# Token halves for the last image's expert scatter, products laid out by group, and new engine orders

## The chip, the cores and the metric

One core of a Trainium2 chip runs the whole program in one launch. The metric is device time in microseconds (us), lower is better. TensorE does matrix products and transposes, VectorE, ScalarE and GpSimd (POOL in the rows) everything else, SyncE issues the DMAs.

## The reference

Four images x of 16 x 16 tokens and 128 channels go through two layers. The first is a deformable attention block. The second is an attention over the tokens with a choice of segments, and then the part that this change touches, a product-key expert layer. Cut to what matters:

```
# second layer, per image: t is 256 tokens x 128 channels, 8 heads
q  = layernorm_per_head(t_ln @ Wq.T + bq)                # 8 heads x 64
s0 = l2norm(q[..., :32]) @ l2norm(keys0).T               # 64 scores
s1 = l2norm(q[..., 32:]) @ l2norm(keys1).T               # 64 scores
sc0, ix0 = top_k(s0, 16);  sc1, ix1 = top_k(s1, 16)
fs, pos  = top_k(all sums sc0 + sc1, 16)                 # 16 chosen pairs
fi = (all sums ix0 + ix1)[pos]                           # expert number, 0 to 126
w  = softmax(fs)
act = gelu(t_ln . expert_down[fi])
t  = t + sum over heads and chosen of (act * w) * expert_up[fi]
```

Expert numbers are sums of two indices below 64, so only 128 experts occur.

## The kernel before

Each engine has its own in-order list of steps in `ORDERS`; a step has a name and an image, as N3a.2. A string `BANKS` gives each PSUM result its bank, in the order in which TensorE makes them. Engines meet through semaphores (a bank full, a bank free, a tile ready). The steps A and F of an image are the first layer and the attention of the second, the steps N its expert layer. The lists interleave the expert layer of image b with the front of image b+1 and b+2. An image has 256 tokens in two halves t = 0, 1 of 128.

The expert layer of an image, in the order of its data:

- N0a, N0h (halves 0, 1): queries, their squares (ScalarE), variances (VectorE), the power -0.5 (POOL, L1573). N0b, N0d: normalized queries, transposed. N0c, N0e: key scores (TensorE L775), copied to S (ScalarE L1045). N0f, N0g: norms.
- N1_0 to N1_3: VectorE finds the best 16 of 64 with MAX8, MATCH_REPLACE8 and FIND_INDEX8.
- N2p, N2q, N2a to N2f: sums, exponentials and the choice of 16 (halves 0, 0, 0, 1, 1, 1 on VectorE in N2a, N2b, N2c, N2d, N2e, N2f). `chosen` ends N2c and N2f with the sum, its reciprocal (L1388) and that times `W_SCALE` = 2^15 (L1389). POOL's `merge` puts weights and expert numbers into 27 slots per head and multiplies the weights by the scaled reciprocal (L1620), in N2c and N2f.
- N3a: TensorE transposes both halves' slots into banks wT and eT (8 transposes, 4 heads by 27 slots = 108 rows), once `slots_ready` counts both halves. ScalarE copies them to W2 (float16) and eT (uint16). VectorE takes the low 2 and the high 5 bits of the expert number (L1419, L1420), the float16 remainder of the weights (L1425), four masks for the low bits (L1428), and the products of weights and masks, R (L1432).
- N3b: the one-hots OH for the 32 values of the high bits, 28 on VectorE (L1437) and 4 on POOL (L1647), each over all 512 columns (2 chunks of heads, 2 halves, 4 x 32 tokens).
- N5a, N5b: the scatter, 128 small products each, OH by R (TensorE L839), into banks G0 and G1, one per token half. VectorE multiplies each with the activations of N4 into `prod` (L1442).
- N6a, N6b: 4 products with expert_up (TensorE L850), copy (ScalarE L1098), transpose, add and output (VectorE L1459), DMA.

So in the last image no other work is left after N2f.3 but this chain. The layout of `prod` decides how VectorE writes and how TensorE reads:

```
prod = masked[...].rearrange("p (l t q g) -> p l t q g", l=LO, t=NT, q=4)
# VectorE writes element (g, q, l) of half t; TensorE reads prod[:, lo], 256 elements
```

VectorE's, ScalarE's and POOL's operand tiles for the masks share SBUF: `lom` lies in `cands`, R in `weights`, `prod` in `masked`.

Of the kernel before, what the change touches and what calls it, by code (L numbers as in the profile page):

```python
# [31 lines left out]
NT = 2
# [87 lines left out]
    "scalar": """A0b.0 A1a.0 A2c.0 A2d.0 A3a.0 A1b.0 A3b.0 A3c.0 A4.0 A0b.1 F5b.0 A1a.1 F5c.0 F6b.0 F7a.0 F7b.0 A2c.1  # L120
        F8a.0 F8b.0 A1b.1 A2d.1 F9a.0 A3a.1 A3b.1 A3c.1 A4.1 A0b.2 F8c.0 F10a.0 F10b.0 F11t.0 A1a.2 F11b.0 F5b.1
        F12.0 F5c.1 N0a.0 F6b.1 N0h.0 N0b.0 N0c.0 F7a.1 F7b.1 N0d.0 F8a.1 F8b.1 A2c.2 F8c.1 N2p.0 A2d.2 F9a.1
        N0e.0 A3a.2 A3b.2 A3c.2 N2q.0 A1b.2 F10a.1 A4.2 F10b.1 F11t.1 F11b.1 N3a.0 F5b.2 F12.1 F5c.2 N0a.1 N0h.1
# [1598 lines left out]
```

## Time and profile before

| | us |
|---|---|
| median of 3 runs | 472.86 (471.47 to 474.82) |
| profiled execution, its own time | 472.43 |
| its span in the trace | 470.6 |
| mean granted TensorE clock, share of full | 0.675 |
| VectorE busy | 356.8 |
| TensorE busy | 296.5 |
| POOL busy | 220.8 |
| ScalarE busy | 137.3 |

The time of the profiled execution is 1.8 us more than its span. Busy times are sums over an engine's instructions; what an engine waits for is read from the chain and from the idle times.

### The profile page before, as it was taken

What the parts mean: (1) busy time and instruction counts of PE and PEld (TensorE: products, weight loads), DVE (VectorE), ACT (ScalarE), POOL (GpSimd) and SP (SyncE); (2) the same over time, 40 slices, a digit from 0 to 9 for tenths busy, and PEclk for the clock granted to TensorE, in tenths of its full rate; (3) what the DMA queues carried; (4) which work ended last, traced back from release to release, by engine and by line L of the source; (5) the groups of instructions that cost most, each with busy time, mean ns of one, the idle gap of its engine ahead of it and who ended that gap; (6) DMA issues with size and microseconds to landing.
All of it is one profiled execution on the core that took longest, in us unless ns stands there. A gap on an engine that the chain in (4) does not pass through costs nothing.

```text
span 470.6 us, 7700 instructions
## 1 busy us (share of the span) xinstructions
PE 296.5 (63%) x2233; PEld 219.8 (47%) x2233; DVE 356.8 (76%) x2124; ACT 137.3 (29%) x320; POOL 220.8 (47%) x407
## 2 busy tenths in 40 slices
PE   3074365886551485999957777998346579241196
PEld 1043144455340343699734445896122378231194
DVE  2858337227999989689999789999997896995811
ACT  3043232636320236261224544224043202031000
POOL 6229922395262187368455645031633920486300
PEclk9997577857685577575695975558758656575555
DMA  6000000000000000000000000000000000000000
GB/s 211 0 0 1 1 1 0 1 1 0 2 0 1 1 2 1 1 3 2 1 1 1 13 1 0 2 3 1 1 1 12 0 2 1 1 2 11 0 1 13
DMA packets 1633, 3.50 MB, mean 7 GB/s; under 512 B 180, under 2 KB 1205, under 8 KB 1592
## 3 DMA queue, kind: packets, MB, share of 16 engines
q1 hardware_dynamic: 1592, 3.01, 1.8%
q8 instruction: 18, 0.29, 0.3%
q14 instruction: 23, 0.19, 0.1%
HBM read 2.49 MB, written 0.52 MB: 6 GB/s over the span
## 4 chain that ended last, share of the span: by engine, by line
DVE 49%; PE 33%; ACT 7%; issue 5%; POOL 5%; DVEq 0%; ACTq 0%; POOLq 0%
PE bank L839 9%; DVE cands L1376 4%; DVE segmax L1201 4%; PE bank L520 4%; DVE onehot L1437 3%; DVE Sx L1320 3%; PE bank L755 3%; PE bank L775 3%; DVE i L1326 3%; DVE i L1327 3%; DVE c L1373 3%; DVE vraw L1323 2%; DVE rtm L1193 2%; DVE vraw L1317 2%; PE bank L608 2%
## 5 line engine op out<-in xcount | busy, mean ns | idle before, releaser
L839 PE MATMUL bank<-weights,onehot 108*128 108x16 f16 x1024 | 68.6, 216 | 18.5 <-DVE onehot L1437 13.0
L839 PEld LDWEIGHTS bank<-weights,onehot 108*128 108x128 f16 x1024 | 68.7, 175 | 19.4 <-DVE onehot L1437 13.5
L1584 POOL TENSOR_TENSOR inv<-nrm,mhalf 128x16 f32<-128x16 f32 x8 | 24.2, 3019 | 46.9 <-DVE nrm L1333 46.8
L454 POOL TENSOR_TENSOR taps<-qpad,wa 128x128 f32<-128x128 f32 x96 | 35.9, 425 | 17.4 <-ACT qpad L892 17.4
L1497 POOL TENSOR_TENSOR rstd<-veps,mhalf 128x2 f32<-128x2 f32 x16 | 11.7, 729 | 44.0 <-DVE veps L1123 43.7
L1647 POOL TENSOR_SCALAR onehot<-eT 108x512 f16<-108x512 uint16 x16 | 30.2, 1888 | 4.2 <-DVE eT L1420 3.5
L1437 DVE TENSOR_SCALAR onehot<-eT 108x512 f16<-108x512 uint16 x112 | 28.1, 327 | 0.0
L1326 DVE FIND_INDEX8 i<-vraw,S 128x8 uint16<-128x64 f32 x128 | 28.0, 219 | 0.0
L1327 DVE FIND_INDEX8 i<-vraw,Sx 128x8 uint16<-128x64 f32 x128 | 28.0, 219 | 0.0
L708 PE MATMUL bank<-qB,kE 32*128 32x256 f32 x128 | 16.3, 663 | 18.0 <-ACT PT L1003 10.1
L775 PE MATMUL bank<-KB,qsT 128*128 128x256 f32 x64 | 24.4, 548 | 3.5 <-ACT qsT L1035 3.5
L1320 DVE MATCH_REPLACE8 Sx<-vraw,S 128x64 f32<-128x64 f32 x128 | 25.1, 209 | 0.0
L1573 POOL TENSOR_TENSOR qrstd<-ssq,mhalf 128x8 f32<-128x8 f32 x8 | 17.7, 2212 | 14.7 <-DVE ssq L1285 14.7
L1376 DVE MATCH_REPLACE8 cands<-c,cands 128x54 f32<-128x54 f32 x128 | 23.7, 199 | 0.0
L520 PE MATMUL bank<-wa,hat 128*128 128x128 f32 x24 | 7.4, 406 | 24.8 <-ACT hat L877 24.6
L1317 DVE MAX8 vraw<-S 128x8 f32<-128x64 f32 x128 | 17.7, 213 | 6.3 <-ACT S L1045 6.3
L1201 DVE TENSOR_REDUCE segmax<-bank 128x32 f32<-128x512 f32 x32 | 19.8, 681 | 2.5 <-PE bank L678 2.4
L775 PEld LDWEIGHTS bank<-KB,qsT 128*128 128x128 f32 x64 | 17.2, 283 | 8.1 <-ACT qsT L1035 4.9
L1602 POOL TENSOR_TENSOR weights<-ab 128x64 f32<-128x64 f32 (+3 forms) x40 | 12.6, 348 | 17.9 <-ACT ab L1065 17.9
L1529 POOL TENSOR_TENSOR taps<-taps 128x1536 f32<-128x1536 f32 (+3 forms) x12 | 20.6, 1714 | 0.6
L1442 DVE TENSOR_TENSOR masked<-bank,act 128x512 f32<-128x512 f32 x8 | 8.4, 1072 | 16.0 <-PE bank L839 15.9
L708 PEld LDWEIGHTS bank<-qB,kE 32*128 32x128 f32 x128 | 10.0, 319 | 22.1 <-issue 12.0
(224 smaller groups left out, 775.9 us busy)
## 6 DMA issues: line engine op xcount, KB each, us to landing
wa<-wa_dram SPq DMA_DIRECT2D x1, 747.5 KB, 4.6
wb<-wb_dram SPq DMA_DIRECT2D x1, 707.0 KB, 5.7
x_sb<-x_dram SPq DMA_DIRECT2D x4, 128.0 KB, 4.0
out_dram<-eT SPq DMA_DIRECT2D x4, 128.0 KB, 1.7
onehot<-ws_dram SPq DMA_DIRECT2D x1, 448.0 KB, 6.3
bq_row<-rows_dram SPq DMA_DIRECT2D x1, 0.5 KB
onehot<-rows_dram SPq DMA_DIRECT2D x1, 13.5 KB
```

The lines of the kernel that those rows point to most:

```text
L454: ins = eng.tensor_tensor(tv[:, :, :, ky, kx:kx + n], q, dw[:, ky, kx:kx + n].unsqueeze(1).unsqueeze(1).broadcast_to([P, G8, G8, n]), ALU. ...
L708: last = mm(banks[i][:, kc * N:kc * N + N], kE[r, j, kc * P:kc * P + P], qB[r, j, :], start=True, stop=True)
L775: last = mm(o[:, i * 256:i * 256 + 256], qsT[:, t, 2 * j + i, :], KB[:, :], start=True, stop=True)
L839: last = mm(o[:, g * 16:g * 16 + 16], OHv[:, c * NT + t, g], Rv[:, c, t, g, s], start=(c == 0 and s == 0), stop=(c == NCH - 1 and s == 1))
L1201: freed(v.tensor_reduce(segmax[:, t * H + i:t * H + H:4, :], o[:, :].rearrange("p (g n) -> p g n", n=SEG), X, ALU.max), job, b)
L1317: last = v.max(vt[:, g, 0:8], sv[:, g, :])
L1320: last = v.match_replace(sx[:, g, :], vt[:, g, 0:8], sv[:, g, :], MARK)
L1326: v.max_index(it[:, g, 0:8], vt[:, g, 0:8], sv[:, g, :])
L1327: last = v.max_index(it[:, g, 8:16], vt[:, g, 8:16], sx[:, g, :])
L1376: last = v.match_replace(dst[:, g, :], c8[:, g, i, :], src[:, g, :], MARK)
L1437: last = v.tensor_scalar(OH[0:KC, :, :, hi, :], hi_view(eT), float(LO * hi), None, ALU.is_equal)
L1647: last = g_.tensor_scalar(OH[0:KC, :, :, hi, :], hi_view(eT), float(LO * hi), None, ALU.is_equal)
```

## The change

1. In the last image N3a and N3b work on token half 0 alone, and new steps N3h (transposes, copies, bits, masks, R) and N3i (one-hots) on half 1. N3a.3 waits for one half's slots, N5a.3 for half 0's one-hots, N5b.3 for half 1's. R is then made with 8 instructions a half (each of the two float16 parts alone) instead of 4 in all. The other images keep whole steps.
2. The scale 2^15 moves from its own VectorE instruction into ScalarE's copy (the function Identity with a scale for Copy) and into the subtraction, which becomes one scalar_tensor_tensor.
3. `prod` is laid out by half, group and (q, l): VectorE writes 512 elements in a row, TensorE reads with a step of 16 elements.
4. All four orders and the banks are new.

```diff
+    "N3a": ["wT", "eT"], "N3h": ["wT1", "eT1"],
     "N4": ["I"],
     "N5a": ["G0"], "N5b": ["G1"],
...
-        F12.2 N0a.2 N0h.2 F6a.3 F6b.3 N0b.2 F6c.3 N0f.2 N0c.2 N0d.2 N0e.2 N5a.1 F7a.3 F7b.3 N5b.1 F8a.3 N4.2
...
-        F12.3 N0a.3 N0h.3 N0b.3 N0c.3 N0f.3 N5a.2 N0d.3 N0e.3 N0g.3 N5b.2 N6a.2 N4.3 N6b.2 N3a.3 N5a.3 N5b.3
-        N6a.3 N6b.3""".split(),
...
-        N6a.1 F11t.3 F11b.3 N3a.2 F12.3 N0a.3 N0h.3 N0b.3 N0c.3 N0d.3 N0e.3 N2p.3 N2q.3 N6a.2 N4.3 N3a.3 N6a.3""".split(),
...
-        N3a.2 N0a.3 N0h.3 N0b.3 N3b.2 N1_0.3 N0d.3 N1_1.3 N1_2.3 N0f.3 N5a.2 N1_3.3 N0g.3 N2a.3 N5b.2 N2d.3
-        N2b.3 N2c.3 N2e.3 N2f.3 N6b.2 N3a.3 N3b.3 N5a.3 N5b.3 N6b.3""".split(),
...
-        N0f.2 N2a.2 N0g.2 N2c.2 N2d.2 N2f.2 F11c.3 N0a.3 N0h.3 N3b.2 N0f.3 N0g.3 N2a.3 N2d.3 N2c.3 N2f.3 N3b.3""".split(),
...
+        F12.2 N0a.2 F6a.3 N0h.2 F6b.3 N0b.2 F6c.3 N0c.2 N0f.2 N5a.1 F7a.3 N0d.2 F7b.3 N0e.2 N5b.1 F8a.3 F8b.3
...
+        F12.3 N0a.3 N0h.3 N0b.3 N0c.3 N5a.2 N0d.3 N0f.3 N0e.3 N5b.2 N0g.3 N4.3 N6a.2 N6b.2 N3a.3 N3h.3 N5a.3
+        N5b.3 N6a.3 N6b.3""".split(),
...
+        F10b.3 F11t.3 F11b.3 N3a.2 F12.3 N0a.3 N0h.3 N0b.3 N0c.3 N0d.3 N0e.3 N2p.3 N2q.3 N4.3 N6a.2 N3a.3 N3h.3
+        N6a.3""".split(),
...
+        N0a.3 N0h.3 N0b.3 N3b.2 N1_0.3 N0d.3 N1_1.3 N1_2.3 N0f.3 N1_3.3 N0g.3 N5a.2 N5b.2 N2a.3 N2b.3 N2d.3
+        N2c.3 N6b.2 N2e.3 N2f.3 N3a.3 N3b.3 N3h.3 N3i.3 N5a.3 N5b.3 N6b.3""".split(),
...
+        F7b.3 N2a.2 N2c.2 N0g.2 N2d.2 N2f.2 F11c.3 N0a.3 N3b.2 N0h.3 N0f.3 N0g.3 N2a.3 N2d.3 N2c.3 N2f.3 N3b.3
+        N3i.3""".split(),
...
-        prod = masked[:, 0:NT * 32 * 4 * LO].rearrange("p (l t q g) -> p l t q g", l=LO, t=NT, q=4)
+        prod = masked[:, 0:NT * 32 * 4 * LO].rearrange("p (t g e) -> p t g e", t=NT, g=32)
...
+        def first_halves(b):
+
+            return list(range(NT)) if b < B - 1 else [0]
+
+        def part(ap, halves):
+
+            return ap if len(halves) == NT else ap.rearrange("p (c t n) -> p c t n", c=NCH, t=NT)[:, :, halves[0], :]
+
+        def masks(unit, hi, halves):
+
+            e = eT[0:KC, 2, :]
+            if len(halves) == NT:
+                return unit.tensor_scalar(OH[0:KC, :, :, hi, :], e.rearrange("p (n q g) -> p n q g", n=NCH * NT, q=4),
+                                          float(LO * hi), None, ALU.is_equal)
+            t = halves[0]
+            return unit.tensor_scalar(OH[0:KC, t:NCH * NT:NT, :, hi, :],
+                                      e.rearrange("p (n q g) -> p n q g", n=NCH * NT, q=4)[:, t:NCH * NT:NT],
+                                      float(LO * hi), None, ALU.is_equal)
...
+                read_out(pe, "tT", b)
...
+            def slot_transposes(b, halves, job):
+                pe.wait_ge(slots_ready, NT * b + halves[-1] + 1)
+                for kind, src in (("w", wn[:, :, :]), ("e", slots[:, 1, :, :])):
+                    transposes(kind + job, b, [
+                        ((c * NT + t) * P, src[:, t * H + c * HC:t * H + (c + 1) * HC, :].rearrange("p h s -> p (h s)"))
+                        for c in range(NCH) for t in halves])
+
             def N3a(b):
-                pe.wait_ge(slots_ready, NT * (b + 1))
-                for job, src in (("wT", wn[:, :, :]), ("eT", slots[:, 1, :, :])):
-                    transposes(job, b, [((c * NT + t) * P,
-                                         src[:, t * H + c * HC:t * H + (c + 1) * HC, :].rearrange("p h s -> p (h s)"))
-                                        for c in range(NCH) for t in range(NT)])
+                slot_transposes(b, first_halves(b), "T")
+
+            def N3h(b):
+                slot_transposes(b, [1], "T1")
...
             def N5b(b):
+                if b == B - 1:
+                    pe.wait_ge(onehot_dve_ready, b + 2)
+                    pe.wait_ge(onehot_pool_ready, b + 2)
                 scatter(b, 1)
...
+                pv = prod[:, :, :, :].rearrange("p t g (q l) -> p l t q g", q=4)
                 for lo in range(LO):
-                    last = mm(o[:, 0:N], up[:, lo, :], prod[:, lo], start=(lo == 0), stop=(lo == LO - 1))
+                    last = mm(o[:, 0:N], up[:, lo, :], pv[:, lo], start=(lo == 0), stop=(lo == LO - 1))
...
+            def slot_copies(b, halves, job):
+                o = full(ac, "w" + job, b)
+                link(fn(part(W2[0:KC, 0, :], halves), part(o[0:KC, :], halves), ACT.Identity, scale=W_SCALE))
+                o = full(ac, "e" + job, b)
+                freed(fn(part(eT[0:KC, 0, :], halves), part(o[0:KC, :], halves), ACT.Copy), "e" + job, b)
...
-                o = full(ac, "wT", b)
-                link(fn(W2[0:KC, 0, :], o[0:KC, :], ACT.Copy))
-                o = full(ac, "eT", b)
-                freed(fn(eT[0:KC, 0, :], o[0:KC, :], ACT.Copy), "eT", b)
+                slot_copies(b, first_halves(b), "T")
+
+            def N3h(b):
+                slot_copies(b, [1], "T1")
...
-                link(v.reciprocal(zs[:, 1, h], zs[:, 0, h]))
-                v.tensor_scalar(zs[:, 2, h], zs[:, 1, h], W_SCALE, None, ALU.mult).then_inc(wem_ready, 1)
+                v.reciprocal(zs[:, 1, h], zs[:, 0, h]).then_inc(wem_ready, 1)
...
+            def slot_rows(b, halves, job):
+                n = b + halves[-1] if b == B - 1 else b
+                read_out(dve, "e" + job, b)
+                v.tensor_scalar(part(eT[0:KC, 1, :], halves), part(eT[0:KC, 0, :], halves), LO - 1, None, ALU.bitwise_and)
+                v.tensor_scalar(part(eT[0:KC, 2, :], halves), part(eT[0:KC, 0, :], halves), E - LO, None,
+                                ALU.bitwise_and).then_inc(eT_ready, 1)
+
+                o = full(dve, "w" + job, b)
+                dve.wait_ge(act_chain, n + 1)
+                freed(v.scalar_tensor_tensor(part(W2[0:KC, 1, :], halves), part(o[0:KC, :], halves), W_SCALE,
+                                             part(W2[0:KC, 0, :], halves), ALU.mult, ALU.subtract), "w" + job, b)
+                dve.wait_ge(eT_ready, n + 1)
+                for lo in range(LO):
+                    last = v.tensor_scalar(part(lom[0:KC, lo, :], halves), part(eT[0:KC, 1, :], halves), float(lo), None,
+                                           ALU.is_equal)
+                link(last)
+                read_out(dve, "w" + job, b)
+                for lo in range(LO):
+                    if len(halves) == NT:
+                        v.tensor_tensor(R[0:KC, :, lo, :], W2[0:KC, :, :],
+                                        lom[0:KC, lo, :].unsqueeze(1).broadcast_to([KC, 2, NCH * N]), ALU.mult)
+                    else:
+                        for s in range(2):
+                            v.tensor_tensor(part(R[0:KC, s, lo, :], halves), part(W2[0:KC, s, :], halves),
+                                            part(lom[0:KC, lo, :], halves), ALU.mult)
...
+                slot_rows(b, first_halves(b), "T")
+
+            def N3h(b):
+                slot_rows(b, [1], "T1")
...
+                    last = masks(v, hi, first_halves(b))
+                last.then_inc(onehot_dve_ready, 1)
+
+            def N3i(b):
+                for hi in range(POOL_HI, HI):
+                    last = masks(v, hi, [1])
                 last.then_inc(onehot_dve_ready, 1)
...
                 freed(v.tensor_tensor(
-                    prod[:, :, t, :, :].rearrange("p l q g -> p g q l"),
-                    o[:, :].rearrange("p (g q l) -> p g q l", g=32, q=4), act[:, t, :, :, :], ALU.mult), f"G{t}", b)
+                    prod[:, t, :, :], o[:, :].rearrange("p (g e) -> p g e", g=32),
+                    act[:, t, :, :, :].rearrange("p g q l -> p g (q l)"), ALU.mult), f"G{t}", b)
...
-                                 zs[:, 2, h].unsqueeze(2).broadcast_to([P, H, SLOTS]), ALU.mult)\
+                                 zs[:, 1, h].unsqueeze(2).broadcast_to([P, H, SLOTS]), ALU.mult)\
...
+                    last = masks(g_, hi, first_halves(b))
+                last.then_inc(onehot_pool_ready, 1)
+
+            def N3i(b):
+                pool.wait_ge(eT_ready, b + 2)
+                for hi in range(0, POOL_HI):
+                    last = masks(g_, hi, [1])
                 last.then_inc(onehot_pool_ready, 1)
```

Entries of a list that an engine has no code for (as A2b.0 on POOL) do nothing. The other differences of the lists are exchanges of near neighbours: POOL takes N0a.0 and N0h.0 before the taps of image 2, ScalarE does A1a.2 after F12.0, and TensorE does N0d.2 and N0e.2 behind N5a.1, where both stood before it.

## Rows read from the trace of the kernel before

**Rows 1.** The page of the whole span: slices and chain by engine

```profile
DVE  2858337227999989689999789999997896995811
PEclk9997577857685577575695975558758656575555
...
DVE 49%; PE 33%; ACT 7%; issue 5%; POOL 5%; DVEq 0%; ACTq 0%; POOLq 0%
```

**Rows 2.** The timeline, all engines, end of the last image's choice (start, us, what)

```profile
424.63 1.32 POOL L1620 TENSOR_TENSOR wn<-slots,zs 128x216 f32<-128x216 f32 x1
...
426.45 0.17 DVE L1389 TENSOR_SCALAR zs<-zs 128x8 f32<-128x8 f32 x1
426.53 0.42 DVE L1459 TENSOR_TENSOR eT<-bank,t 128x256 f32<-128x256 f32 x1
```

**Rows 3.** The timeline, all engines, from the last slots to the end

```profile
429.21 0.55 POOL L1620 TENSOR_TENSOR wn<-slots,zs 128x216 f32<-128x216 f32 x1
...
431.03 0.60 ACT L1082 ACTIVATE W<-bank 108x512 f16<-108x512 f32 x1 [9.70 <-PE bank L520]
...
432.56 0.29 DVE L1419 TENSOR_SCALAR eT<-eT 108x512 uint16<-108x512 uint16 x1 [5.60 <-ACT eT L1084]
...
433.21 6.54 POOL L1647 TENSOR_SCALAR onehot<-eT 108x512 f16<-108x512 uint16 x4 [3.46 <-DVE eT L1420]
...
438.20 6.55 DVE L1437 TENSOR_SCALAR onehot<-eT 108x512 f16<-108x512 uint16 x28
...
444.80 16.98 PE L839 MATMUL bank<-weights,onehot 108*128 108x16 f16 x256 [13.04 <-DVE onehot L1437]
...
461.82 1.02 DVE L1442 TENSOR_TENSOR masked<-bank,act 128x512 f32<-128x512 f32 x1 [7.07 <-PE bank L839]
...
462.95 3.75 PE L850 MATMUL bank<-masked,up 128*128 128x256 f32 x8 [1.16 <-issue]
466.74 0.38 ACT L1098 ACTIVATE W<-bank 128x256 f32<-128x256 f32 x1 [34.28 <-PE bank L850]
...
467.97 0.42 DVE L1459 TENSOR_TENSOR eT<-bank,t 128x256 f32<-128x256 f32 x1 [5.12 <-PE bank L520]
```

**Rows 4.** Windows of N3a.1, N3b.2, N3b.1: busy us (x count) of PE, PEld, DVE, ACT, POOL

```profile
271.30:275.80 4.50, 3.56 (x7) 1.19 (x8) 4.45 (x12) 2.63 (x6) 0.00 (x0) 0.75 0.00 2
...
367.40:373.20 5.80, 4.76 (x17) 3.77 (x17) 5.80 (x30) 2.18 (x4) 5.80 (x2) 0.56 0.00 0
...
280.00:289.10 9.10, 8.04 (x26) 5.88 (x25) 9.10 (x30) 2.99 (x5) 7.33 (x5) 0.52 0.00 0
```

**Rows 5.** The timeline of VectorE in N3a.1 and just before N3a.2

```profile
272.33 0.89 DVE L1428 TENSOR_SCALAR cands<-eT 108x512 f16<-108x512 uint16 x4
273.25 2.50 DVE L1432 TENSOR_TENSOR weights<-W,cands 108x1024 f16<-108x1024 f16 x4
...
358.22 0.17 DVE L1122 TENSOR_SCALAR negmean<-mv 128x2 f32<-128x2 f32 x1
358.30 0.16 DVE L1123 TENSOR_SCALAR veps<-mv 128x2 f32<-128x2 f32 x1
```

**Rows 6.** Groups by line and shape, VectorE: count, then busy us, mean ns

```profile
L1442 DVE TENSOR_TENSOR masked<-bank,act 128x512 f32<-128x512 f32 x8 | 8.4, 1072 | 16.0 <-PE bank L839 15.9
L1291 DVE TENSOR_TENSOR queries<-bank,qrstd 128x512 f32<-128x512 f32 x8 | 5.5, 683 | 1.1 <-POOL qrstd L1573 1.1
...
L1389 DVE TENSOR_SCALAR zs<-zs 128x8 f32<-128x8 f32 x8 | 1.5, 182 | 0.3
```

**Rows 7.** The timelines of POOL, TensorE and VectorE around the scatter of image 2

```profile
368.61 10.58 POOL L1647 TENSOR_SCALAR onehot<-eT 108x512 f16<-108x512 uint16 x4
...
379.29 8.56 PE L839 MATMUL bank<-weights,onehot 108*128 108x16 f16 x128 [5.51 <-issue]
...
392.46 1.11 DVE L1317 MAX8 vraw<-S 128x8 f32<-128x64 f32 x8 [4.50 <-ACT S L1045]
```

**Rows 8.** Groups by line and shape, TensorE's weight loads

```profile
L839 PEld LDWEIGHTS bank<-weights,onehot 108*128 108x128 f16 x1024 | 68.7, 175 | 19.4 <-DVE onehot L1437 13.5 <-issue 5.8
```

More of the change, by code:

```diff
@@ L120 @@
[L120 to L123, printed above, removed]
-        A0b.3 F6b.2 N0b.1 N0c.1 N0d.1 A1a.3 N4.0 F7a.2 N0e.1 F7b.2 F8a.2 F8b.2 F8c.2 F9a.2 A2c.3 A2d.3 N2p.1
-        A3a.3 A3b.3 A3c.3 F10a.2 F10b.2 N2q.1 A1b.3 F11t.2 N6a.0 A4.3 F11b.2 F5b.3 N3a.1 F12.2 F5c.3 N0a.2 N0h.2
-        F6b.3 N0b.2 N0c.2 N0d.2 N4.1 F7a.3 F7b.3 N0e.2 F8a.3 N4.2 F8b.3 F9a.3 N2p.2 N2q.2 F10a.3 F8c.3 F10b.3
-        N6a.1 F11t.3 F11b.3 N3a.2 F12.3 N0a.3 N0h.3 N0b.3 N0c.3 N0d.3 N0e.3 N2p.3 N2q.3 N6a.2 N4.3 N3a.3 N6a.3""".split(),
@@ new lines @@
+    "vector": """A0a.0 NB.0 A2c.0 A3a.0 A0a.1 F5a.0 NS.0 F6a.0 F6c.0 F7b.0 A2c.1 F8b.0 F9b.0 F9a.0 F9c.0 A0a.2 F9d.0
+        F5a.1 F11a.0 F11c.0 N0a.0 F6a.1 N0b.0 N0h.0 F6c.1 N0d.0 N1_0.0 N1_1.0 F7b.1 N0f.0 N0g.0 N1_2.0 A2c.2
+        N2a.0 F8b.1 N1_3.0 F9b.1 A3a.1 F9a.1 F9c.1 N2b.0 F9d.1 N2d.0 N2c.0 N2e.0 N2f.0 F11a.1 A0a.3 F11c.1 F5a.2
+        N3a.0 N3b.0 N0a.1 A3a.2 F6a.2 N0h.1 N0b.1 N0d.1 F6c.2 N1_0.1 N1_1.1 N0f.1 N1_2.1 F7b.2 N2a.1 A2c.3 N2b.1
+        N5a.0 N5b.0 F8b.2 F9b.2 F9a.2 F9c.2 N2c.1 F9d.2 N0g.1 N1_3.1 N2d.1 N2e.1 A3a.3 N2f.1 F11a.2 N6b.0 F5a.3
+        F11c.2 N3a.1 N0a.2 F6a.3 N0b.2 N3b.1 N0h.2 N1_0.2 F6c.3 N0d.2 N1_1.2 N5a.1 F7b.3 N0f.2 N1_2.2 N2a.2
+        N2b.2 F8b.3 N5b.1 F9b.3 F9a.3 F9c.3 N2c.2 N0g.2 F9d.3 N1_3.2 N2d.2 N2e.2 N2f.2 F11a.3 N6b.1 F11c.3 N3a.2
+        N0a.3 N0h.3 N0b.3 N3b.2 N1_0.3 N0d.3 N1_1.3 N1_2.3 N0f.3 N1_3.3 N0g.3 N5a.2 N5b.2 N2a.3 N2b.3 N2d.3
+        N2c.3 N6b.2 N2e.3 N2f.3 N3a.3 N3b.3 N3h.3 N3i.3 N5a.3 N5b.3 N6b.3""".split(),
@@ L860, in _ @@
                   "F10b": F10b, "F11a": F11a, "F11t": F11t, "F11b": F11b, "F11c": F11c, "F12": F12, "NS": NS,
-                  "N0a": N0a, "N0h": N0h, "N0b": N0b, "N0c": N0c, "N0d": N0d, "N0e": N0e, "N0f": N0f, "N0g": N0g, "N3a":
-                  N3a, "N4": N4, "N5a": N5a, "N5b": N5b, "N6a": N6a, "N6b": N6b}
+                  "N0a": N0a, "N0h": N0h, "N0b": N0b, "N0c": N0c, "N0d": N0d, "N0e": N0e, "N0f": N0f, "N0g": N0g, "N3a": N3a, "N3h": N3h, "N4": N4, "N5a": N5a, "N5b": N5b, "N6a": N6a, "N6b": N6b}
             for s, b in schedule("tensor"):
@@ L1468, in _ @@
                   N1_1, "N1_2": N1_2, "N1_3": N1_3, "N2a": N2a, "N2b": N2b, "N2c": N2c, "N2d": N2d, "N2e": N2e,
-                  "N2f": N2f, "N3a": N3a, "N3b": N3b, "N5a": N5a, "N5b": N5b, "N6b": N6b, "NB": setup_rows}
+                  "N2f": N2f, "N3a": N3a, "N3b": N3b, "N3h": N3h, "N3i": N3i, "N5a": N5a, "N5b": N5b, "N6b": N6b, "NB": setup_rows}
             for s, b in schedule("vector"):
```

72 lines of the change are left out of this document (26 added, 46 removed).

## The prediction

> **What bounds the kernel now.** I read the chain of waits first, then the timeline of the last 50 us, then windows and groups for prices. The chain gives VectorE 49% of the span and TensorE 33%; VectorE's slices are nearly full from the tenth on and empty again in the last four [rows 1]. So there are three regimes. Up to about 100 us a latency chain through image 0's front, then some 320 us in which VectorE is almost always at work, then the tail, where only the last image is left.
>
> The tail is a queue of steps of which each waits for the whole of the one before. VectorE ends N2f.3 at 426.62 (426.45 + 0.17) [rows 2]. POOL's last weights are there at 429.76, VectorE starts N3a.3 at 432.56, ends the one-hots at 444.75, TensorE scatters for 16.98 us alone, from 444.80 to 461.78, and product, up-projection and output end at 468.39 [rows 3]. From N2f.3's end to the scatter's end it is 461.78 - 426.62 = 35.16 us. During VectorE's 12.2 us TensorE is idle, during the scatter VectorE is, and the first half's weights lay ready from 425.95 (424.63 + 1.32) [rows 2]. TensorE's granted clock is about half in these slices [rows 1], the lower of its levels; nothing in the change raises it, so I keep the scatter's price.
>
> **The change, part by part.** T is the end of N2f.3 on VectorE, 426.62 before.
>
> *Start of half 0.* Between the last weights and N3a.3 lay 432.56 - 429.76 = 2.80 us for 8 transposes and two ScalarE copies of 512 [rows 3]. With 4 transposes and copies of 256 (0.38 as L1098 instead of 0.60 as L1082 [rows 3], so 0.44 less for two) and about 0.6 less transposing (half of the 1.27 us from 429.76 until the first copy starts at 431.03) it is 1.8. Half 0's weights come 0.67 before T, and N6b.2, 0.42 long [rows 2], now stands between N2c.3 and N2e.3, so 1.1 before T. VectorE starts half 0 at T + 0.7 and waits that long for it. The bounds are 0.1 (transposes all hidden) and 2.1 (nothing gets shorter and N6b.2 adds no lead).
>
> *VectorE's work for one half.* Undisturbed, the whole N3a takes 4.45 us [rows 4], of it 0.92 for the four low masks (272.33 to 273.25) and 2.42 for the four R [rows 5]; the 28 one-hots take 5.8 us at most, 0.205 each (the window of N3b.2, of which 0.06 are neighbours) [rows 4]. What an instruction costs without elements is near 0.08, the distance of two two-element ones [rows 5]. Then a one-hot of 256 columns is 0.08 + 0.0625 = 0.142, 28 of them 4.0; a low mask 0.155, four 0.6; an R of 256 instead of 1,024 elements 0.08 + 0.13 = 0.21, eight 1.7; the bits and the remainder, 1.03 whole (271.30 [rows 4] to 272.33 [rows 5]), about 0.65. That is 7.0 us, against half of 10.2 = 5.1 if there were no fixed cost, and 10.2 if nothing shrank. I take 7.0, because the two-element rows show the fixed cost.
>
> *POOL beside it.* N3b.1's window is 9.1 us with POOL's four masks in it, N3b.2's, 5.8, has the same 28 one-hots on VectorE and little of POOL's finished [rows 4]; before, N3a.3 and N3b.3 together took 12.2 with 6.54 us of POOL masks beside them [rows 3], 2.0 more than 10.2. So POOL's masks cost VectorE 2 to 3.3 us whole. For half 0 POOL now has its merge of half 1 (3.1 us, from T to 429.76) and half masks beside VectorE. I add 1.5, between 0.5 and 4.2. N5a.3 starts at T + 0.7 + 7.0 + 1.5 = T + 9.2.
>
> *The scatter.* 16.98 / 2 = 8.5 for half 0 [rows 3]. Half 1's work on VectorE, 7.0 + 1.0 beside POOL's second masks, begins at T + 9.2 and ends at T + 17.2, half 0's scatter at T + 17.7. So half 1 is hidden with only 0.5 us to spare, and N5b.3 ends at T + 26.2. Before it was T + 35.2. The split gives 9.0; with POOL's and the start's bounds 5 to 11.
>
> *Products.* L1442 takes 1.07 us; L1291, also one PSUM input, one SBUF input, 512 float32 and a result in a row, takes 0.683 [rows 6]. The difference, 0.39, is what the result's step costs, if it is the step. The last product is on the end of the path: 0.4. TensorE then reads `prod` with 64-byte steps, in L850's 3.75 us. OH (float16) is loaded with a step of 64 bytes too, 128 columns in 175 ns on average, most of it beside other work [rows 8]: such a load and its product together take 16.98 / 256 = 0.066 us [rows 3], far less than the 0.47 us of one L850 instruction (3.75 / 8) for 256 columns. I take zero, up to 3.75 if reads took twice as long.
>
> The Trainium skill (SBUF — State Buffer, Specifications) says that each access to a new 16-byte line pays a penalty and that two hits on a line are wanted. By it the write of the product becomes cheaper, which agrees with 1,072 against 683 ns, but all of TensorE's reads for N6a pay; no row here shows by how much for float32.
>
> *Scale.* L1389, 0.182 mean [rows 6], goes 8 times, 7 of them ahead of T; the eighth releases POOL. Identity for Copy and scalar_tensor_tensor for tensor_tensor process the same elements from the same places: nothing, up to 0.1 each.
>
> *Before T.* VectorE sheds 8 x 0.18 = 1.4 and the six products of images 0 to 2, 6 x 0.39 = 2.3, together 3.7. It is not always the limit (VectorE waits 4.5 us before N1_2.3 [rows 7], and waits elsewhere end with an engine that hasn't become faster), so I count half, 1.9, between 0 and 3.7.
>
> *Orders.* One exchange has a row. TensorE was idle 5.51 us before N5a.2 until POOL's last mask at 379.19, which stood behind N0h.3, and N0d.3 and N0e.3 queued behind that scatter; VectorE waited 4.50 us for their scores [rows 7]. Now POOL does N3b.2 before N0h.3. It can gain up to 4.5, or nothing where VectorE's own masks hold POOL up as they did (10.58 us for four [rows 7], against 7.33 of POOL in all in image 1's window [rows 4]); I take 1.0. N6b.2 ahead of T costs 0.4. For all other exchanges and banks I take 0, with -6 to +4: they move steps by a few places, and the removed waits in a full VectorE are only worth what VectorE idles.
>
> T moves from 426.6 by -1.9 - 1.0 + 0.4 = -2.5.
>
> **Sum.** 2.5 + 9.0 + 0.4 = 11.9 us. The profiled execution, 472.43, would become 460.5; it lies 0.4 below the median 472.86, so on the median it is 461.0.
>
> **The rivals.**
>
> *A. The lock.* POOL and VectorE don't slow each other but take turns. For it speaks that image 2's POOL masks took 10.58 us while VectorE made its own [rows 7]; against it, that in N3b.1 one-hots worth 5.7 us and 7.33 of POOL fitted into 9.1 [rows 4], where turns would need nearly 13. In turns half 0 needs 7.0 plus 3.3 of masks (half of 6.54) plus about 2.4 of merge, 4.2 more than I counted, and half 1 needs 10.3 against a scatter of 8.5, 1.8 more. Then 461.0 + 6.0 = 467.0. The Trainium skill (SBUF — State Buffer, Who interferes with whom) states this as a rule: an exclusive lock for a whole instruction, taken by tensor_scalar in its fast modes or by two SBUF inputs. The trace agrees that there is a price, not that all is serial.
>
> *B. Better orders.* VectorE's idle in the first 110 us and the 4.5 us go down by 4 more: 457.0. For it, every removed idle there counts; against, that stretch is a chain through all engines.
>
> *C. A shared wait.* N5a.3 or VectorE's half 0 waits for something of half 1, so the split gives nothing and the doubled fixed costs (2 x 7.0 - 10.2 = 3.8) fall due: 461.0 + 9.0 = 470.0 to 473.8. In the code N5a.3 waits for counts b+1 and N3a.3 for the first half, so this is unlikely; I put it at 471.
>
> *D. Strided reads.* N6a.3 doubles: 461.0 + 3.75 = 464.8.
>
> *E. Slower: scatters in VectorE's way.* In the new TensorE list N0d.2 and N0e.2 stand behind N5a.1 and F7a.3. A scatter is 8.5 us in which key scores queue, and the trace shows one such case, at 4.5 us of VectorE idle [rows 7]. If two scatters fall wholly into VectorE's way it is 461.0 + 17.0 = 478.0. It decides once N0e's scores are later than N1_1's end by more than 12 us in sum, 473. Against it, VectorE has N1_0.2 and N1_1.2, 128 searches and more, queued to cover one scatter.
>
> **How the numbers follow.** Forecast 0.62 (457.5 to 464.5), A 0.13, B 0.10, D 0.05, C 0.05, E 0.05. A tenth of the chance lies below about 457 and a tenth above 468, so the range is 455.5 to 468. A change of under 1% (4.7 us) can't be told from none here. Faster by over 1% means under 468.1: forecast, B, D and nearly all of A, 0.89. Within 1% are C and A's upper end, 0.07; slower by over 1% is E's larger part, 0.04.
>
> **What would show it.** Right: the scatter's first product within 8 to 10.5 us of N2f.3's end, 256 products without a gap over 0.5 us, POOL's masks of half 1 beside the first 128, L1442 near 0.68 us, no L1389, N6a.3 at 3.7 us, VectorE's wait before N1_2.3 shorter. Wrong: one-hots of 256 columns at over 0.2 us, a gap between the halves of the scatter, or a VectorE idle of several us at a place that had none in images 1 and 2.

## Result and the profile after

| | before | after |
|---|---|---|
| median of 4 runs, us | 473.58 (471.47 to 474.82) | 457.69 (457.07 to 460.12) |
| profiled execution, its own time | 472.43 | 460.12 |
| its span | 470.6 | 458.0 |

The ratio is 0.9679, with a 95% interval of 0.9626 to 0.9731: 15.2 us less than before (12.7 to 17.7). The profiled execution after is the longest of its four. In all comparisons the medians take every execution, and the ratios leave out one of e9's six, a slow one of 457.0 us at a lower granted clock; e8 has three slow ones of six, and its ratio fits all six.

The page after answers to [rows 1]. The first two lines are the span and VectorE's busy tenths, then the granted clock in tenths, then the chain by engine.

```profile
span 458.0 us, 7753 instructions
...
DVE  4828328225999998849999978999998699999950
...
PEclk9997556787567577555678589555785665665556
...
DVE 57%; PE 22%; POOL 7%; issue 7%; ACT 5%; DMA 0%; DVEq 0%; POOLq 0%; ACTq 0%
```

VectorE now has 57% of the chain and TensorE 22%, where it was 49% and 33%, so more of the chain that ended last runs over VectorE. VectorE's digits are near full up to the third slice from the end, and the last but one holds a 5, its work on half 1 beside the scatter. The granted clock of the last slices is 0.5 to 0.6, as before.

The timeline of the tail answers to [rows 2] and [rows 3]. T, the end of N2f.3 on VectorE, is 423.40 + 0.20 = 423.60.

```profile
421.27 0.55 POOL L1671 TENSOR_TENSOR wn<-slots,zs 128x216 f32<-128x216 f32 x1
...
421.58 1.15 DVE L1417 SCALAR_TENSOR_TENSOR masked<-cands,weights 128x864 f32<-128x864 f32 x1
...
423.08 0.38 ACT L1107 ACTIVATE eT<-bank 108x256 uint16<-108x256 f32 x1
423.40 0.20 DVE L1422 RECIPROCAL zs<-zs 128x8 f32<-128x8 f32 x1
423.56 0.23 DVE L1450 TENSOR_SCALAR eT<-eT 108x256 uint16<-108x256 uint16 x1
...
424.22 1.23 DVE L1460 TENSOR_SCALAR cands<-eT 108x256 f16<-108x256 uint16 x4
425.48 2.46 DVE L1470 TENSOR_TENSOR weights<-W,cands 108x256 f16<-108x256 f16 x8
...
426.95 3.83 POOL L495 TENSOR_SCALAR onehot<-eT 108x256 f16<-108x256 uint16 x4
...
427.86 4.82 DVE L495 TENSOR_SCALAR onehot<-eT 108x256 f16<-108x256 uint16 x28
...
432.60 0.22 DVE L1450 TENSOR_SCALAR eT<-eT 108x256 uint16<-108x256 uint16 x1
...
432.74 17.05 PE L867 MATMUL bank<-weights,onehot 108*128 108x16 f16 x256 [4.60 <-DVE onehot L495]
...
433.04 3.85 POOL L495 TENSOR_SCALAR onehot<-eT 108x256 f16<-108x256 uint16 x4 [2.26 <-DVE eT L1451]
433.20 0.85 DVE L1460 TENSOR_SCALAR cands<-eT 108x256 f16<-108x256 uint16 x4
434.09 2.06 DVE L1470 TENSOR_TENSOR weights<-W,cands 108x256 f16<-108x256 f16 x8
436.07 4.22 DVE L495 TENSOR_SCALAR onehot<-eT 108x256 f16<-108x256 uint16 x28
441.45 0.69 DVE L1493 TENSOR_TENSOR masked<-bank,act 128x512 f32<-128x512 f32 x1 [1.17 <-PE bank L867]
449.82 0.69 DVE L1493 TENSOR_TENSOR masked<-bank,act 128x512 f32<-128x512 f32 x1 [7.67 <-PE bank L867]
...
450.61 3.76 PE L879 MATMUL bank<-masked,up 128*128 128x256 f32 x8 [0.83 <-issue]
...
455.39 0.42 DVE L1510 TENSOR_TENSOR eT<-bank,t 128x256 f32<-128x256 f32 x1 [4.88 <-PE bank L538]
```

Read it as two interleaved queues. Half 0's expert numbers arrive in SBUF at 423.08 + 0.38 = 423.46, before T, so VectorE goes from the reciprocal straight into half 0 (423.56). Its one-hots end at 432.68, and TensorE begins its 256 products at 432.74. VectorE turns to half 1 at 432.60 and is done at 440.29. The 256 products then stand in one group without a gap to 449.79. L1493 for half 0 (it was L1442) waits 1.17 us for TensorE, so half 1 was hidden with about that to spare. From T the first product is at +9.1 (before +18.2), the end of the scatter at +26.2 (before +35.2). TensorE's products with `prod` at 64-byte steps (L879, it was L850) take 3.76 us in this tail, against 3.75 [rows 3]; in image 0 they take longer than before (last section).

The 9.0 us that left the tail up to the scatter's end are so made: 5.9 in which VectorE had waited from T until half 1's slots were merged, transposed and copied (432.56 - 426.62), and 3.1 of the 12.2 us of masks [rows 3].

The group of the product with the activations, which answers to the first of [rows 6]:

```profile
L1493 DVE TENSOR_TENSOR masked<-bank,act 128x512 f32<-128x512 f32 x8 | 5.3, 684 | 8.9 <-PE bank L867 8.8
```

1,072 ns has become 684, the price of L1291 beside it in [rows 6].

Image 2's one-hots, N3b.2, in the timeline of POOL and VectorE, which answer to [rows 7]:

```profile
365.78 7.08 POOL L492 TENSOR_SCALAR onehot<-eT 108x512 f16<-108x512 uint16 x4
...
366.45 8.58 DVE L492 TENSOR_SCALAR onehot<-eT 108x512 f16<-108x512 uint16 x28
```

POOL's masks now come first, and VectorE's wait of 4.50 us before N1_2.3 is gone. But VectorE's own 28 masks take 8.58 us. In the kernel before they took 5.74, and there it was POOL that stood, as its timeline and VectorE's show:

```profile
367.00 6.22 POOL L1573 TENSOR_TENSOR qrstd<-ssq,mhalf 128x8 f32<-128x8 f32 x1 [0.49 <-DVE ssq L1285]
...
367.44 5.74 DVE L1437 TENSOR_SCALAR onehot<-eT 108x512 f16<-108x512 uint16 x28
```

POOL's power, 1.64 us elsewhere, took 6.22 and ended at 373.22, with the last of VectorE's masks at 373.18, and POOL's four masks behind it took 10.58 [rows 7] instead of 6.54.

### The profile page after: what moved, and what is told of

Read it like the earlier page. It is cut to its first block, busy times and chain, and to the rows that moved or that the text cites. A ratio compares the mean times of both kernels' runs of the same rounds, so it can differ in the third digit from the quotient of the medians.

```text
span 458.0 us, 7753 instructions
## 1 busy us (share of the span) xinstructions
PE 310.4 (68%) x2233; PEld 230.4 (50%) x2233; DVE 360.6 (79%) x2163; ACT 141.3 (31%) x324; POOL 216.7 (47%) x411
## 4 chain that ended last, share of the span: by engine, by line
DVE 57%; PE 22%; POOL 7%; issue 7%; ACT 5%; DMA 0%; DVEq 0%; POOLq 0%; ACTq 0%
PE bank L867 7%; DVE Sx L1354 5%; DVE cands L1410 5%; DVE i L1360 5%; DVE i L1361 4%; DVE segmax L1235 4%; DVE onehot L492 4%; DVE vraw L1357 3%; DVE c L1407 3%; DVE vraw L1351 3%; PE bank L538 2%; DVE masked L1417 2%; DVE cands L1399 2%; DVE rtm L1227 2%; PE bank L794 2%
## 5 line engine op out<-in xcount | busy, mean ns | idle before, releaser
L794 PE MATMUL bank<-KB,qsT 128*128 128x256 f32 x64 | 25.7, 573 | 1.8 <-ACT qsT L1063 1.7
L1624 POOL TENSOR_TENSOR qrstd<-ssq,mhalf 128x8 f32<-128x8 f32 x8 | 13.6, 1704 | 27.3 <-DVE ssq L1319 27.2
L492 DVE TENSOR_SCALAR onehot<-eT 108x512 f16<-108x512 uint16 x84 | 23.7, 357 | 0.0
L492 POOL TENSOR_SCALAR onehot<-eT 108x512 f16<-108x512 uint16 x12 | 20.2, 1680 | 2.2 <-DVE eT L1451 1.6
L1648 POOL TENSOR_TENSOR ab<-v 128x256 f32<-128x256 f32 x8 | 5.4, 676 | 32.9 <-DVE v L1393 14.1
L1351 DVE MAX8 vraw<-S 128x8 f32<-128x64 f32 x128 | 17.7, 210 | 3.4 <-ACT S L1073 3.4
L1031 ACT ACTIVATE PT<-bank 128x512 f32<-128x512 f32 x32 | 16.3, 613 | 10.4 <-PE bank L727 10.4
L538 PEld LDWEIGHTS bank<-wa,hat 128*128 128x128 f32 x24 | 3.4, 196 | 30.7 <-ACT hat L905 30.7
L1357 DVE MAX8 vraw<-Sx 128x8 f32<-128x64 f32 x128 | 17.8, 211 | 0.6
```

The source lines that it names most:

```text
L492: return unit.tensor_scalar(OH[0:KC, :, :, hi, :], e.rearrange("p (n q g) -> p n q g", n=NCH * NT, q=4), float(LO * hi), None, ALU.is_equal)
L794: last = mm(o[:, i * 256:i * 256 + 256], qsT[:, t, 2 * j + i, :], KB[:, :], start=True, stop=True)
L1351: last = v.max(vt[:, g, 0:8], sv[:, g, :])
L1357: last = v.max(vt[:, g, 8:16], sx[:, g, :])
```

## Experiments

All were timed in rounds with the kernel before on the same chip, one chip for e1 to e4, one for e5 to e8 and one for e9 to e12, with the medians of before in that order. The ratio is to that kernel; 0.01 is 4.7 us. T and "from T" are read from the timeline of the profiled execution, T in us from the span's start: the distances are those of the first product of the scatter, its end, and the end of VectorE's last add.

| kernel | median, us | ratio (95%) | T | from T |
|---|---|---|---|---|
| before | 473.0, 474.2, 475.1 | 1 | 426.6 | 18.2, 35.2, 41.8 |
| after | 457.69 | 0.9679 (0.9626 to 0.9731) | 423.6 | 9.1, 26.2, 32.2 |
| e1 | 468.65 | 0.9865 (0.9818 to 0.9913) | 431.2 | 11.0, 28.0, 34.3 |
| e2 | 465.5 | 0.9832 (0.9774 to 0.9889) | 427.0 | 9.1, 26.2, 32.6 |
| e3 | 467.03 | 0.9828 (0.978 to 0.9876) | 422.2 | 18.2, 35.2, 41.3 |
| e4 | 469.51 | 0.9906 (0.9873 to 0.9939) | 427.3 | 18.2, 35.4, 41.7 |
| e5 | 462.07 | 0.9751 (0.971 to 0.9792) | 425.2 | 9.8, 26.8, 32.9 |
| e6 | 473.38 | 0.9978 (0.9945 to 1.0011) | 428.2 | 18.2, 35.3, 41.9 |
| e7 | 460.43 | 0.9694 (0.9649 to 0.9739) | 424.4 | 9.1, 26.1, 32.5 |
| e8 | 454.38 | 0.9574 (0.9522 to 0.9627) | 412.2 | 8.5, 25.6, 31.6 |
| e9 | 449.1 | 0.9456 (0.9422 to 0.9489) | 412.8 | 9.1, 26.2, 32.2 |
| e10 | 458.35 | 0.9644 (0.9606 to 0.9682) | 421.5 | 9.1, 26.2, 32.3 |
| e11 | 467.36 | 0.9849 (0.9811 to 0.9887) | 425.1 | 16.9, 34.0, 40.4 |
| e12, after again | 457.61 | 0.9634 (0.9599 to 0.9668) | 419.3 | 9.1, 26.2, 32.2 |

Two kinds of number stand in this table. The distances from T repeat within 0.2 us in kernels with the same tail. T itself doesn't: after, e12 and e3 are the same program up to T and have it at 423.6, 419.3 and 422.2, and before and e1 at 426.6 and 431.2. So the tail is read from the profile, and what lies ahead of T from the ratios of whole times.

**e1, the split alone**, with the orders, scale and products of before:

```diff
-  "vector": ... N2b.3 N2c.3 N2e.3 N2f.3 N6b.2 N3a.3 N3b.3 N5a.3 N5b.3 N6b.3
+  "vector": ... N2b.3 N2c.3 N2e.3 N2f.3 N6b.2 N3a.3 N3b.3 N3h.3 N3i.3 N5a.3 N5b.3 N6b.3
```

> The kernel before with the split of the last image alone: N3h and N3i added, all else (scale, product layout, orders, banks) as before, N6b.2 still behind N2f.3. Theory of the split: ScalarE's N3a.3 now has to wait until image 2's output is stored, which VectorE releases 0.3 us after T, so half 0 starts some 3 us later than in the changed kernel: 28.5 to 30 us from the end of N2f.3 (T) to the end of the scatter, where it was 35.2, a span of 464 to 466 us. Rival, the split alone is worth all of its 9 us: 461.6. Rival, the new orders carry the gain: the span stays within 2 us of 470.6.

It gained 6.4 us (4.1 to 8.6) and its scatter ends at T + 28.0, 7.1 earlier than before. VectorE enters N3a.3 only at T + 3.2. Its timeline says why:

```profile
431.57 0.33 SPq L509 DMA_DIRECT2D out_dram<-eT  x1
...
433.44 0.38 ACT L1100 ACTIVATE W<-bank 108x256 f16<-108x256 f32 x1 [7.34 <-DMA out_dram<-eT]
...
434.35 0.23 DVE L1446 TENSOR_SCALAR eT<-eT 108x256 uint16<-108x256 uint16 x1 [2.86 <-ACT eT L1102]
```

ScalarE's copy of half 0 (433.44) had waited 7.34 us, and what ended the wait is image 2's output going out (`out_dram<-eT`): the step's copies fill `eT` again, from which that output is read. With N6b.2 behind N2f.3, the output is late.

**e2, the split and N6b.2 moved** ahead of N2e.3:

```diff
-  "vector": ... N2c.3 N2e.3 N2f.3 N6b.2 N3a.3 N3b.3 N3h.3 ...
+  "vector": ... N2c.3 N6b.2 N2e.3 N2f.3 N3a.3 N3b.3 N3h.3 ...
```

> As the kernel with the split alone, but VectorE does N6b.2 right behind N2c.3. Theory of the split: T + 26.2 at the end of the scatter, less 0.4 for N6b.2 in front of T, a span of 462.0 (461 to 463). Rival, N6b.2's place doesn't matter: the same as the kernel with the split alone. Rival, the new orders carry the gain: above 467.

N3a.3 starts at T and the scatter ends at T + 26.2, as in the kernel after. So the moved step is a condition of the split: it is worth 1.8 us of the 9.0 behind T, less the 0.4 that it now takes ahead of T.

**e3, the kernel after without the split:**

```diff
-            return list(range(NT)) if b < B - 1 else [0]
+            return list(range(NT))
```

> The changed kernel without the split (N3a.3 and N3b.3 whole, N3h and N3i gone); scale, products, orders and banks are the new ones. Theory of the split: T as in the changed kernel, 423.7, the end of the scatter 34 to 35 us later, a span of 466 to 467.5. Rival, the orders carry the gain: 458 to 461.

```profile
428.81 6.54 POOL L488 TENSOR_SCALAR onehot<-eT 108x512 f16<-108x512 uint16 x4 [3.46 <-DVE eT L1444]
...
433.79 6.55 DVE L488 TENSOR_SCALAR onehot<-eT 108x512 f16<-108x512 uint16 x28
...
440.39 17.04 PE L860 MATMUL bank<-weights,onehot 108*128 108x16 f16 x256 [13.04 <-DVE onehot L488]
...
457.48 0.69 DVE L1486 TENSOR_TENSOR masked<-bank,act 128x512 f32<-128x512 f32 x1 [7.63 <-PE bank L860]
```

The queue of before is back: masks, then 256 products after all of them. The scatter ends at T + 35.2, 9.0 later than in the kernel after. By the ratios the split is worth 0.9828 - 0.9679, 7.0 us (3.6 to 10.4), here and 7.9 us (5.3 to 10.7) in e2. Both intervals hold 9.0; the 9.0 itself rests on the distances from T.

**e4, only the scale and the products** on top of before:

> The kernel before with the scale in ScalarE's copy and the products laid out by group, nothing else. By the prediction's terms: 0.4 from the last product and half of 3.7 us ahead of T, a span of 468.3 (466.5 to 470.2). Rival, all of the VectorE time that is saved counts: 466.5. Rival, the waits take it all: 470.2. TensorE's N6a.3 stays at 3.7 us; if reads with a step of 64 bytes were slow it would be 5 to 7.5.

4.4 us faster (2.9 to 6.0), nearly all of it ahead of T, since the tail is that of before but for 0.3 us from the scatter's end to the output's (6.3 for 6.6). N6a.3's reads at the new step take the same time, 3.78 us for 3.75, at a granted clock of 0.50 in both; N6a.0's, at 1.00, take 3.70 where they took 1.99.

**e5, all of the change but the new orders and banks** (N6b.2 still moved):

> The changed kernel with the orders and banks of the kernel before (N3h and N3i added at their places, N6b.2 behind N2c.3). Theory that the orders are worth little: split 8.6, scale and products 2.3, a span of 459.5 to 460.5, 1.5 to 2.5 above the changed kernel, most of it the 4.5 us wait of VectorE before N1_2.3 less what POOL's masks cost VectorE in N3b.2. Rival, the new orders lose time (VectorE is 3 us later until about 265 us in the changed kernel): 455 to 457. Rival, they carry much: above 463.

It lies 0.0072, 3.4 us, above the kernel after, with an uncertainty of 3.2 (the half-widths 0.0041 and 0.0053 added in squares); the intervals overlap a little. Its tail is 0.6 longer, and its timeline says why:

```profile
423.31 1.06 DVE L1413 SCALAR_TENSOR_TENSOR masked<-cands,weights 128x864 f32<-128x864 f32 x1
423.32 1.45 POOL L1667 TENSOR_TENSOR wn<-slots,zs 128x216 f32<-128x216 f32 x1
...
426.53 0.35 DVE L1446 TENSOR_SCALAR eT<-eT 108x256 uint16<-108x256 uint16 x1 [1.28 <-ACT eT L1103]
```

POOL's multiplication of half 0's weights begins in the same moment as VectorE's scalar_tensor_tensor with two SBUF inputs, and takes 1.45 us instead of the 0.55 that it takes in the kernel after (421.27), where it got ahead. The slots of half 0 come that much later, and N3a.3 waits 1.28 us.

**e6, POOL's masks ahead of N0h.3** in before and nothing else:

```diff
-  "gpsimd": ... F11c.3 N0a.3 N0h.3 N3b.2 N0f.3 ...
+  "gpsimd": ... F11c.3 N0a.3 N3b.2 N0h.3 N0f.3 ...
```

> The kernel before with one exchange in POOL's list: N3b.2 ahead of N0h.3. Theory: POOL's masks then run beside VectorE's, which take 8.6 instead of 5.7 us (+2.8), and the wait of 4.5 us before N1_2.3 goes: a span of 469.0 (468.5 to 469.5), 1.6 less. Rival, POOL stays locked out until VectorE is done: 470.6. Rival, all of the 4.5 us is won: 466.

0.9978 with 1 inside the interval: the 1.6 us that were expected can't be told from none, but the rival that all of the 4.5 is won is out. The wait before N1_2.3 is gone, 4.5 us, but N3b.2 costs 2.4 more:

```profile
369.78 6.98 POOL L1647 TENSOR_SCALAR onehot<-eT 108x512 f16<-108x512 uint16 x4
...
371.14 8.18 DVE L1437 TENSOR_SCALAR onehot<-eT 108x512 f16<-108x512 uint16 x28
```

**e7, the kernel after with the old layout of `prod`:**

> The changed kernel with the old layout of the products (VectorE writes with large steps, TensorE reads in a row). Theory: the write's step costs 0.37 us for each of 8 products, one of them in the tail, the others ahead of T where VectorE is nearly always the limit: +1.6 to +2.7 on 458.0. Rival, waits absorb all but the last: +0.4. N6a.3 stays at 3.76 us.

0.7 us above the kernel after, with an uncertainty of 3.3: it can't tell nothing from the whole 2.7 (0.4 in the tail and 2.3 ahead of it). TensorE's N6a.0 takes 2.22 us here, at a granted clock of 0.89.

**e8, no masks on POOL**, VectorE makes all 32 of each image (`POOL_HI = 0`, and POOL's waits and those on POOL go):

> The changed kernel without POOL's four one-hot masks: VectorE makes all 32. Theory of the contention: N3b.1 and N3b.2 on VectorE go from 8.6 us (28 beside POOL) to 32 x 0.205 = 6.6, N3b.0 from 6.5 to 6.6 but N3a.0 from 5.65 to 4.45, the halves of the last image from 4.8 and 4.2 to 4.5 each: about 5 us less work on VectorE ahead of T, a span of 453 to 456. Rival, POOL's masks are a help: 0.8 us more VectorE work per image, a span of 460 to 461.

```profile
416.27 4.42 DVE L495 TENSOR_SCALAR onehot<-eT 108x256 f16<-108x256 uint16 x32
...
423.51 4.44 DVE L495 TENSOR_SCALAR onehot<-eT 108x256 f16<-108x256 uint16 x32
```

All 32 one-hots of a half take VectorE 4.42 us alone; in the kernel after, 28 of them took 4.82 with POOL's four beside them. The ratio is 0.9574, 5.0 us (1.5 to 8.5) below the kernel after. Its six times fall into two groups, 447.8 to 453.2 and 455.6 to 456.1.

**e9, masks on POOL in the last image alone** (and the waits for them to match):

```diff
...
-                for hi in range(POOL_HI, HI):
+                for hi in range(POOL_HI if b == B - 1 else 0, HI):
...
             def N3b(b):
-                if b >= 1:
-                    full(pool, "G1", b - 1)
+                if b < B - 1:
+                    return
```

> The changed kernel with VectorE making all 32 one-hot masks in images 0 to 2, POOL its four only in the halves of the last image. Theory that the gain of dropping POOL's masks lies ahead of the tail: the end of N2f.3 as without any POOL masks, the tail 0.6 us longer (T + 26.1 at the end of the scatter), a time within 1 us of the kernel without POOL masks, some 454 to 455. Rival, the tail gives most of it: near the changed kernel, 457.5.

0.9456 (0.9422 to 0.9489): the fastest, 8.5 us (6.2 to 10.8) below the kernel after on the same chip (e12, 0.9634), and faster than both kernels. Five of its six times lie between 448.4 and 449.9, and the ratio is theirs; the sixth is 457.0. Against e8 the difference is unclear: e8's three shortest times, 447.8, 449.6 and 453.2, lie around e9's, its three others make its ratio larger, and by the tail e9 should be 0.6 us longer.

**e10, image 0's POOL masks later** in POOL's list, behind N0h.1:

```diff
-  "gpsimd": ... F11c.1 N3b.0 A0a.3 A0b.3 N0a.1 N0h.1 A2a.3 ...
+  "gpsimd": ... F11c.1 A0a.3 A0b.3 N0a.1 N0h.1 N3b.0 A2a.3 ...
```

> The changed kernel with N3b.0 later in POOL's list, behind N0h.1 instead of ahead of A0a.3; the masks stay. Theory of the queue: what dropping POOL's masks gives in image 0 is that image 3's layernorm (A0a.3, A0b.3) no longer waits behind 6.5 us of masks, so A1a.3 doesn't hold up TensorE's list; then 2 to 4 us less than the changed kernel, 454 to 456. Theory of the contention alone: VectorE's N3a.0 and N3b.0 go from 5.65 + 6.55 to 4.45 + 5.75, 2.0 us less, and N5a.0 has to wait for POOL until about 202 us, behind the 204 where it starts now: 455.7. Rival, the later masks hold up N5a.0 and the key scores behind it: 458 or more.

The same as the kernel after (0.5 us above e12, give or take 2.4). Both theories had 2 to 4 us less, and neither shows in the time. In the profile VectorE's masks of image 0 do end 2.0 us earlier than in e12 after the same start (188.7 for 190.7), so what was expected of the contention happened there, but it didn't reach the end. What took it back wasn't traced.

**e11, before without masks on POOL:**

> The kernel before, VectorE making all 32 one-hot masks (no POOL masks), nothing else. Theory of the contention: independent of the change, N3b.1 2.4 us shorter, N3a.0 1.2, N3b.2 0.8 longer but N5a.2 no longer waits 5.5 us for POOL, so most of the 4.5 us wait of VectorE goes, and in the last image 12.2 becomes 11.0: 6 to 8 us less, 465 to 467. Rival, POOL's masks are a help there: 473 or more.

7.2 us faster than before (5.4 to 9.0), and VectorE's wait before N1_2.3 is gone here too. The removed masks are worth about as much without the change as with it.

**e12, the kernel after again**, beside e9 to e11:

> The changed kernel once more, unchanged, beside these on the same chip: 457 to 459. If programs that are alike up to N2f.3 end it some us apart from run to run, this one's N2f.3 may end anywhere within 3 us of 423.7, while its tail (T + 26.1 at the end of the scatter) repeats within 0.2.

0.9634, against 0.9679 in the first comparison; with 457.61 and 457.69 the medians are the same.

**Where e9 gains.** I compared stretches of its profile with those of e12, the same program otherwise. VectorE's one-hots of images 1 and 2 take 6.55 us each, against 8.32 and 8.18: 3.4 us. In image 0, VectorE's first search of image 1 (N1_0.1) starts 3.0 earlier. The timeline of POOL's masks, of VectorE's and of that search's start, with its wait for the key scores in brackets, in e12, and then VectorE's 32 one-hots and the same start in e9:

```profile
179.16 6.54 POOL L492 TENSOR_SCALAR onehot<-eT 108x512 f16<-108x512 uint16 x4 [1.38 <-DVE eT L1451]
...
184.14 6.55 DVE L492 TENSOR_SCALAR onehot<-eT 108x512 f16<-108x512 uint16 x28
...
192.04 3.25 POOL L1624 TENSOR_TENSOR qrstd<-ssq,mhalf 128x8 f32<-128x8 f32 x2
...
199.72 1.11 DVE L1351 MAX8 vraw<-S 128x8 f32<-128x64 f32 x8 [2.30 <-ACT S L1073]
```

```profile
182.90 6.56 DVE L492 TENSOR_SCALAR onehot<-eT 108x512 f16<-108x512 uint16 x32
...
196.68 1.11 DVE L1351 MAX8 vraw<-S 128x8 f32<-128x64 f32 x8 [0.39 <-ACT S L1074]
```

2.30 us of wait (2.99 in the first profile of the kernel after) against 0.39. Of the 3.0, 1.2 are VectorE's own: N3a.0 starts at 178.57 and 178.51, and the one-hots end at 190.69 in e12 and at 189.46 in e9, because without POOL's masks beside them the low masks take 0.89 us for 1.34 and R 2.50 for 3.26. POOL begins the deviations of image 1's queries, on which the scores wait, at 192.04 and 190.80, 1.2 apart too. The other 1.8 arise behind that, where TensorE's granted clock was higher in e9 as well (below), and how much of them is the clock's is open; in e11, against before, this search wasn't earlier. 3.4 + 3.0 = 6.4 of the 8.5 us, and T is 6.5 earlier; the rest is not in this pair of profiles.

## Why the prediction was right

Forecast 461.0, measured 457.69, in the range, at the lower edge of the 457.5 to 464.5 that the forecast alone was given. The gain was 15.2 us and not 11.9. The mechanism of the tail was the forecast one and its sum was right to 0.1, in part by luck, since two of its terms were off and cancelled. The terms ahead of T were too small by 3.1.

| step | forecast | measured |
|---|---|---|
| half 0 starts | T + 0.7 | T - 0.04 |
| half 0 on VectorE, with POOL | 7.0 + 1.5 = 8.5 | 9.1 |
| first product | T + 9.2 | T + 9.1 |
| half 1 on VectorE, with POOL | 7.0 + 1.0 = 8.0 | 7.7 |
| scatter | 2 x 8.5, no gap | 17.05, no gap |
| end of scatter | T + 26.2 | T + 26.2 |
| L1442 / L1493, mean | 0.68 | 0.684 |
| last product | 0.4 | 0.33 (1.02 to 0.69) |
| reads of `prod` | 0 (to 3.75) | 0.01 in the tail, 1.7 in image 0 |
| before T, in all | 2.5 | about 5.6 (3.1 to 8.1) |

- **The split.** 9.0 forecast, 9.0 in the tail from e3 to the kernel after and 8.9 from before to e2. Two of its parts were off and cancelled. Half 0 began 0.7 earlier, because POOL's multiplication of [rows 2] was taken at 1.32 us, and it takes 0.55 where it gets ahead of VectorE's scalar_tensor_tensor. And half 0 took 0.6 longer than 8.5: POOL's 1.5 was too little. Undisturbed, in half 1 of e8, the low masks take 0.62 us and R 1.71 (forecast 0.6 and 1.7), 28 one-hots would take 3.9 (forecast 4.0) and the half 6.8 (forecast 7.0). In half 0 of the kernel after, beside POOL's merge and masks, low masks, R and one-hots take 1.23, 2.46 and 4.82, so POOL costs VectorE 2.3 us; in half 1, beside the masks alone, 0.85, 2.06 and 4.22, which is 0.9 (forecast 1.0). The fixed cost of an instruction was sized rightly: in e8 a one-hot of 256 columns takes 4.42 / 32 = 0.138 us (forecast 0.142). Without the fixed cost, the 5.1 that I set aside, the forecast would have been 2 us too early.
- **N6b.2.** I charged 0.4 for moving it and credited 0.4 of lead for POOL. e1 and e2 show that behind T the move is worth 1.8 us for another reason: the step's output must leave `eT` before ScalarE may fill it. What the step releases had not been looked up.
- **Scale and products.** "I count half, 1.9" failed: with the last product 0.4, that makes 2.3, and e4 measured 4.4 (2.9 to 6.0), the whole of the 3.7 + 0.4 that VectorE sheds. VectorE is nearly full in images 1 and 2 [rows 1], so that what it sheds arrives is likely, but only argued: e7 can't tell the products' share.
- **Orders.** 1.0 less 0.4, and zero for the rest, was too little: e5 to the kernel after is 3.4 us, give or take 3.2, of it 0.6 in the tail. e6 shows the mechanism of the exchange that I priced: 4.5 us of wait go and 2.4 come back as masks side by side. I had named only that VectorE's masks may hold POOL up, and not that POOL's would lengthen VectorE's. Which of the other exchanges gain is open.
- **The sum** ahead of T: 15.2 in all, less the tail's 9.6 (41.8 - 32.2), is 5.6. Of the 9.6, 9.0 are the split, 0.3 the last product, and nearly all of the rest the last two transposes, 0.69 us before and 0.44 after; they have 0.69 in e4 and 0.44 in e11 too, so that isn't the change. The parts, 7.9 (e2), 4.4 (e4) and 3.4 (orders), add up to 15.7, but each has an uncertainty of 1.5 to 3.2.

**The rivals.** A, turns: half 0 would have needed 4.2 more. VectorE took 4.82 us for 28 one-hots beside POOL's 3.83 and would take 3.9 alone, so about 1 us of POOL's 3.8 falls on VectorE, and A's price is refuted. That the two never stand for each other is not: in image 2 of before, and of e1, e2, e4 and e5 with the same list, POOL stood while VectorE made its 28 masks in 5.74, and where VectorE pays it pays in whole instructions (last section). What decides who stands is not shown. The Trainium skill (SBUF — State Buffer, Who interferes with whom) says that who has the shared pair has it for the whole instruction and the other blocks; the pair of e5 (1.45 against 0.55 us, beside 1.06) agrees with it, the sum of VectorE's masks beside POOL's does not. C is refuted by the rows of the tail. D, slower strided reads, is refuted for the tail, where TensorE is at its lower level, but at full clock the reads do nearly double (last section); whether that costs the kernel time isn't shown, and e7, with the old layout, is the same as the kernel after within 3.3 us. E, scatters in VectorE's way: VectorE's longest wait between 110 us and T is 2.99 in the profile after, and the total rules 478 out. B, that orders would give 4 more, came true in part: its 457.0 is nearer to 457.69 than the forecast is, and the orders gave 3.4 (0.2 to 6.6) where I had 0.6.

**What I had not asked** is whether POOL's masks pay at all. The rows were there: 28 undisturbed at 0.205 each [rows 4], so 0.82 for the four more, against 2 to 3.3 us that I counted as their price to VectorE. I used that price for the last image and not as a question about the others.
